# GNN layer on one core: the high parts of h in f16, made by ScalarE or by GpSimd

## What is computed

```python
h = maximum(layernorm(x), 0)
m = h[src] + edge_attr                    # 206250 x 96
aggr = segment_sum(m, dst, 6250)
out = x + (1 + eps) * h + relu(aggr @ W1 + b1) @ W2 + b2
```

## Time and profile before

| | us |
|---|---|
| three timed runs, median | 525.16 |
| lowest and highest | 523.21 and 527.09 |
| the profiled execution | 525.82 |
| its span in the trace | 523.9 |

### The profile page before, as it was taken

The page is one execution under the profiler, slowest core; times in us unless marked ns, Lnnn a source line. Parts: engine busy times, 40 slices in busy tenths (PEclk is TensorE's granted clock), DMA queues, the critical chain, the costliest instruction groups (busy, mean ns, idle before and its releaser), DMA issues.

```text
span 523.9 us, 22551 instructions
## 1 busy us (share of the span) xinstructions
PE 469.9 (90%) x9174; PEld 446.9 (85%) x9174; DVE 482.8 (92%) x727; ACT 414.3 (79%) x637; POOL 299.4 (57%) x188
## 2 busy tenths in 40 slices
PE   0525789999999999999999999999999999999994
PEld 0414688999899899999999999999999999998994
DVE  7998999999999999989999998899999999999870
ACT  0798777788888887888888788888888888886861
POOL 1330000788888888687888888888888881000000
PEclk9999999999999999999999999999999999999998
DMA  6769888998889987999998789999888887765000
GB/s 204 246 210 251 248 239 243 265 251 225 210 218 237 293 228 177 259 239 277 220 231 212 181 219 254 276 246 229 209 221 191 212 216 187 201 194 148 6 9 21
DMA packets 96867, 110.03 MB, mean 210 GB/s; under 512 B 68900, under 2 KB 70552, under 8 KB 96630
## 3 DMA queue, kind: packets, MB, share of 16 engines
q1 hardware_dynamic: 74854, 98.39, 63.1%
q0 software_dynamic: 21904, 10.13, 15.2%
HBM read 102.00 MB, written 6.48 MB: 207 GB/s over the span
## 4 chain that ended last, share of the span: by engine, by line
PE 77%; DVE 8%; SPq 6%; issue 4%; ACT 3%; DMA 1%; DVEq 0%; ACTq 0%
PE agg_ps L1085 31%; PE oct_ps L1073 22%; PE agg_ps L1079 14%; PE key_ps L1097 5%; PE mlp_ps L1102 4%; SPq L374 3%; DVE lo_hot L595 2%; ACT adj L917 2%; DVE z L595 1%; SPq L375 1%; SPq L373 1%; PE key_ps L1090 1%; DVE hot L602 1%; DMA gathered_edges<-in_dst 1%; ACT hid L930 1%
## 5 line engine op out<-in xcount | busy, mean ns | idle before, releaser
L917 ACT ACTIVATE adj<-oct_ps 128x784 f16<-128x784 f32 x360 | 299.5, 865 | 74.8 <-PE oct_ps L1073 70.6
L524 POOL DMA_INDIRECT gathered_edges<-h_rows,gather_src x144 | 264.5, 1837 | 48.6 <-issue 41.8
L1085 PE MATMUL agg_ps<-hl,adj 128*128 128x192 f16 x2205 | 232.9, 246 | 0.6 <-issue 0.3
L595 DVE TENSOR_TENSOR lo_hot<-iota_z,key 128x2048 f16<-128x2048 f16 x180 | 219.0, 1217 | 0.0
L1073 PE MATMUL oct_ps<-z,lo_hot 128*128 128x98 f16 x2880 | 190.7, 209 | 15.6 <-DVE lo_hot L595 7.8
L1073 PEld LDWEIGHTS oct_ps<-z,lo_hot 128*128 128x128 f16 x2880 | 164.3, 99 | 19.1 <-issue 8.2
L1085 PEld LDWEIGHTS agg_ps<-hl,adj 128*128 128x128 f16 x2205 | 173.5, 97 | 3.1 <-ACT adj L917 0.7
L595 DVE TENSOR_TENSOR z<-z_marks,key 128x1568 f16<-128x1568 f16 x180 | 173.9, 966 | 0.4 <-PE oct_ps L1073 0.4
L1079 PE MATMUL agg_ps<-edges,hot 128*32 128x96 f32 x3240 | 77.5, 250 | 2.3 <-DVE hot L748 2.3
L1079 PEld LDWEIGHTS agg_ps<-edges,hot 128*32 128x32 f32 x3240 | 68.0, 111 | 7.7 <-DVE hot L748 2.6
L486 POOL DMA_INDIRECT win<-packed_keys,row_i x23 | 26.8, 1166 | 68.4 <-DMA gathered_edges<-in_edge_attr 61.8
(11 more groups left out here) (145 smaller groups left out, 186.3 us busy)
## 6 DMA issues: line engine op xcount, KB each, us to landing
edges<-in_edge_attr SPq DMA_DIRECT2D x180, 432.0 KB
gathered_edges<-in_edge_attr SPq DMA_DIRECT2D x16, 432.0 KB
dst<-in_dst SPq DMA_DIRECT2D x180, 4.5 KB
gathered_edges<-h_rows,gather_src POOLq DMA_INDIRECT x144
out<-ob SPq DMA_DIRECT2D x45, 48.0 KB
packed_keys<-adj SPq DMA_DIRECT2D x1, 1632.0 KB, 6.0
h_rows<-gathered_edges SPq DMA_DIRECT2D x1, 1200.0 KB, 9.2
h_rows<-gathered_edges SPq DMA_DIRECT2D x1, 1152.0 KB, 8.4
```

The source lines that it names most:

```text
L524: nc.gpsimd.indirect_dma_start(out=gathered[k][:, g, t, :], out_offset=None, in_=h_dram, in_offset=bass.IndirectOffsetOnAxis(ap=gather_src ...
L595: return nc.vector.tensor_tensor(out.rearrange("p t (w two) -> p t w two", two=2), marks[0:out.shape[0], 0:width].rearrange("p (o w two) - ...
L917: return nc.scalar.activation(adj[k][:, :, 2 * OCT * o:2 * OCT * (o + 1)].rearrange("p h (t q) -> p t h q", q=2), oct_ps[:, o % 2, :].rear ...
L1085: last = nc.tensor.matmul(agg_ps[buf][:, 0:2 * C], adj[buf][:, h, :], hl[:, h, :], start=False, stop=(h == NT - 1), skip_group_check=True)
```

## The change

The two activations at L941 are taken out of ACT's queue. POOL makes the same values with `tensor_scalar` (one tensor input, f32, times 4096, output f16), the first before `fetch(WINS)` and the second behind it. The waits for `h_ready` and the signal `high_ready` move with them. The program of DVE, PE and SP is the same.

```diff
@@ block.gpsimd
             fetched = WINS + 1
-            fetch(WINS)
+            for k in range(2):
+                pool.wait_ge(h_ready, k + 1)
+                nc.gpsimd.tensor_scalar(hl[:, ROWS[k], 0:C], h_sb[:, ROWS[k], :], SCALE, None, ALU.mult).then_inc(high_ready, 1)
+                if k == 0:
+                    fetch(WINS)
             pool.wait_ge(h_stored, 32)
@@ block.scalar
-            def high_part(k):
-                act.wait_ge(h_ready, k + 1)
-                nc.scalar.activation(hl[:, ROWS[k], 0:C], h_sb[:, ROWS[k], :], ACT.Copy, scale=SCALE).then_inc(high_ready, 1)
-
...
                 if t + 1 == KEYS_AFTER:
                     next_keys(0)
-                if t + 1 == HALF:
-                    high_part(0)
             last.then_inc(h_ready, 1)
-            high_part(1)
```

## The result

The changed kernel has a median of 530.44 us over 20 runs (528.54 to 533.32), the kernel before 526.25 us over 20 runs (522.42 to 530.61). The ratio is 1.0088 with a 95% interval of 1.0070 to 1.0106. That ratio makes 4.6 us; the two medians lie 4.2 us apart. The forecast was 525.2 us and no change, in a range up to 528.4 us. It was wrong, and the case that came is the mechanism of rival (a), at a price of the instruction above all that were considered there.

What follows compares the result with a forecast made beforehand. Block 3's `dst` ids landing before L762 at 68.20 us were taken to bound the stretch; ACT -4.31, POOL +4.48, DVE +3.09 us of stalls left 0.0 at path end, so 525.2 us, range 522.6 to 528.4 us.

Steps and rivals of the forecast that it cites:

- rival (a): POOL is slow and DVE's stalls exceed their cover: 528.0 us at the two-input price, 530.0 us at twice DVE's; chance 0.12.
- What bounds the stretch: Before the long regular part, the landing of block 3's `dst` ids ends last, holding DVE's L762 until 68.20 us.
- What is removed from ACT: Two activations of 2.11 and 2.20 us; the first gains nothing, the second brings ACT's octets 2.11 us sooner.
- What is added to POOL: Two scalings on a free POOL, priced from casts at 2.20 and 2.28 us, with 4.10 and 4.27 us as high price.
- My high bound: POOL price at the rate of two-input L496, 1.78 ns a column: 4.10 and 4.27 us.
- What it does to DVE: POOL's instructions stall DVE's two-input work, L609 by 0.81 us and again near 45.33 us; 3.09 us of stalls together.
- the prediction's formula: DVE reaches L739 at 44.52 + 5.51 + (d - 1.39) + d us, losing only what lies beyond 54.23 us.
- The cover: DVE's idle time before its waits, 2.70 us at L739 and 0.96 us at L762, absorbs the stalls.
- break-even: Loss begins when one high part on POOL takes d = 2.8 us, 1.2 ns a column.
- SP does not answer: SP reaches the two stores of h only at 42.34 and 53.62 us, after `h_ready`, so its loads stay put.
- Its dearest case: POOL at twice DVE's pass, 5.1 and 5.3 us: loss 4.8 us, 530.0 us; chance 0.03 near that price or beyond.
- The chances: Whole kernel: within 1% (5.25 us) 0.95, slower by more 0.03, faster by more 0.02.

Runs made afterwards that it cites:

- price run: Kernel before plus ten extra POOL instructions that leave the output unchanged, two beside DVE, eight with other engines idle; scaling 6.03 us, copy 2.10 us.
- the copy: Changed kernel with a plain copy to f16 on POOL in place of the scaling, without the factor 4096; ratio 1.0003 to the kernel before.
- the two-input form: Changed kernel with a two-input multiplication by a constant tile of 4096 on POOL in place of the scaling; ratio 1.0061 to the kernel before.
- the second part alone: Kernel before with only the second high part moved to POOL, the first staying on ACT; ratio 1.0012.
- the first part only: Kernel before with only the first high part moved to POOL, the second staying on ACT; ratio 1.0025.

## Why the prediction was wrong, step by step

- **What bounds the stretch**: right. Without ACT's second copy the wait for the ids took up the gain (4.34 us in place of 0.96, of which 0.9 us is a later landing).
- **What is removed from ACT**: right. 2.1 to 2.4 us sooner at `keep` without the second copy; the first copy stood in a wait for DVE's variance.
- **What is added to POOL: the failed step.** The term "2.20 and 2.28 us" measured 6.06 and 7.00 us. At the rate of the first the second would have taken 6.3 us; I read the other 0.7 us as its wait for DVE's running L599 (it started at 48.24 us, L599 ended at 49.1 us). I took the price of a scaling from rows of copies, because both have one input tile. The price run shows that the number of inputs was the wrong likeness: copies 2.10 us, arithmetic 4.03 to 6.03 us, with the one-input scaling the dearest. The only other row of the right operation, L508 at one column, gives no rate. My high bound, the two-input L496, was not a bound either: it is an integer subtraction, and the float multiplication of two tiles took 5.04 us. Of the range's rows none had the operation of the change at a size that tells its rate; the range had to reach further up for that.
- **What it does to DVE**: the mechanism was right, and the inference from L609's 0.39 us with it. The places (L609, L762 of block 1) were right, and `bn_stats` was undisturbed (2.79 us for 17, as before). Each stall is somewhat shorter than the reckoning gives for the measured instruction: with 6.03 and 6.28 us the prediction's formula puts block 3 at 44.52 + 5.51 + 4.64 + 6.28 - 54.23 = 6.7 us late, the traces say 5.1. DVE's held instruction ended 0.4 to 0.5 us ahead of the end that the trace gives the scaling (38.08 against 38.49 us, 54.73 against 55.24 us); beside the copy and the two-input form it did not (48.48 against 48.40 us, 37.00 against 36.95 us). No run shows why.
- **The cover**: right. With the second part alone, 5.38 us of stall made block 3 late by 1.0 us, so 4.4 us were covered, where the rows give 4.20. The break-even worked out at d = 2.8 us lies between the copy (2.1 us, ratio 1.0003) and the multiplication (5.0 us, 1.0061); no run comes closer to it.
- **"SP does not answer"**: right up to block 3; the stores were issued at 42.52 and 53.63 us, as before. Behind it SP waited 4.3 us for PE's edge sums ahead of the load of block 5, so the loads, too, moved with the delay.
- **Rival (a)** named the mechanism and had 0.12. Its dearest case, twice DVE's own pass, 5.1 and 5.3 us, is nearest to what came. That its 4.8 us of loss lie so near the measured 4.6 us is partly luck: the scaling took 6.03 us, 2.4 times DVE's two-input pass over the same tile (2.55 us), and shorter stalls than the formula's made up for it. The Trainium skill (GPSIMD Engine Reference, "Key points") calls DVE "structurally ~2× faster" for elementwise work, which pointed the right way. The Trainium skill's "roughly line-rate" for one input (GPSIMD Engine Reference, "Engine selection") holds here for the copies (2.10 us, 0.91 ns a column) and not for the scaling (2.6 ns).
- **The chances**: slower by over 1% had 0.03; the ratio is 1.0088, and its interval reaches over 1%. The range ended at 528.4 us, 2.0 us under the measured median. Of the 5.2 us between forecast and median, 1.1 us is the kernel before itself, whose median moved from 525.16 us over three runs to 526.25 us over twenty; its runs lie up to 4.4 us off that median, not 1.95.

**What stays open.** Block 3 is late by 5.1 us, and the ratio makes 4.6 us; with the first part only it is 3.1 us against 1.3 (at most 2.8), with the two-input form 4.1 against 3.2. The intervals of the change (3.7 to 5.6 us) and of the two-input form (1.6 to 4.8 us) hold the delay of block 3; that of the first part just fails to. The traces show where the two part. From block 3 to block 12 the delay of the changed kernel is constant. At the wait for the ids of block 13 it moves, and not the same way each time. These are `rel` of block 13 in the changed kernel, first measurement and second (in the kernel before: 171.48 us after 2.26 us of waiting):

```profile
176.07 0.23 DVE L766 TENSOR_TENSOR rel<-dst,gbase 128x72 f16<-128x72 int32 x1 [1.25 <-DMA dst<-in_dst]
```

```profile
177.57 0.23 DVE L766 TENSOR_TENSOR rel<-dst,gbase 128x72 f16<-128x72 int32 x1 [2.87 <-DMA dst<-in_dst]
```

With the starts taken off, the delay went from 5.1 to 4.1 us in the first and from 5.1 to 5.8 us in the second, and at the last block, after more such waits, it is 4.3 and 7.5 us. So one trace does not show that delay is given back: when the later ids land differs between executions of the same kernel by microseconds. The place of block 3 measures the mechanism, and only the repeated times measure the cost. Why the first part alone cost less than its 3.1 us at block 3 stays open.

## What to carry to other kernels

Price a moved instruction by a row of the same operation, not of the same number of inputs or bytes; where none exists at a size that gives its rate, the unknown price is the widest term of the range. A short run of that one instruction settles it. Work given to GpSimd because it is idle is not free when it reads SBUF: each microsecond of it can stop VectorE's two-input instructions, so what counts is its duration against the idle time that VectorE has there (here 4.2 us against 9.5). And before counting a gain on a side engine, look which transfer or wait ends last behind it: here 2.1 us saved on ScalarE were worth nothing measurable.

## What the runs showed of the hardware

- GpSimd, 128 partitions, 2304 columns, all else idle: `tensor_scalar` multiply 6.03 us whether f16 or f32 out, strided or contiguous; copy or cast 2.10 to 2.11 us; int32 subtraction of two tiles 4.03 us; beside DVE, the f32 multiplication of two tiles to f16 took 5.04 us.
- A GpSimd instruction that reads SBUF held DVE's next instruction with two SBUF inputs, by 0.58 to 5.46 us in the changed kernel and its variants, about as long as it still ran (up to 0.8 us less). A memset of 2.02 us held nothing, and `bn_stats` with one input ran undisturbed beside the reading ones. The Trainium skill (SBUF — State Buffer, "Who interferes with whom") states the same for reading and writing instructions, and these traces agree.
- The hold seems to go both ways. Started while a two-input DVE instruction ran, the scaling over 2400 columns took 7.00 us against the 6.28 us of its rate, the two-input form 6.01 against 5.25 us, and the copy 2.92 against 2.19 us. In all three 0.7 to 0.8 us came on top, and the start in the trace lies before it.
